# Value products of an attention kernel: parts of values side by side, parts of probabilities in one stream, row sums on VectorE

## The reference

```
lat = layer_norm(latents, ln_lat_g, ln_lat_b)
ctx = layer_norm(context, ln_ctx_g, ln_ctx_b)
q = (lat @ Wq).reshape(b, n, HEADS, DHEAD).transpose(0, 2, 1, 3)
kv = ctx @ Wkv
k, v = jnp.split(kv, 2, axis=-1)
...
k = apply_rope(k, cos[None, None], sin[None, None])
attn = jnp.einsum('bhnd,bhsd->bhns', q, k) * scale
attn = jnp.clip(attn, -11.0, 11.0)
attn = jax.nn.softmax(attn, axis=-1)
out = jnp.einsum('bhns,bhsd->bhnd', attn, v)
```

## Time and profile before

| | before |
|---|---|
| median of 3 runs | 1448.81 us (1445.45 to 1450.21) |
| profiled execution, its own time | 1454.4 us |
| its span in the profile | 1452.7 us |
| TensorE busy | 1394.5 us (96%) |
| VectorE busy | 850.0 us (59%) |
| ScalarE busy | 797.3 us (55%) |
| GpSimd busy | 833.6 us (57%) |
| TensorE's granted clock over the run | 0.98 |

### The profile page before, as it was taken

One profiled execution on the slowest core, in us unless ns is written; L12 is line 12 of the kernel. 1 busy time (PEld: TensorE's weight loads), 2 busy tenths in 40 slices (PEclk: granted clock), 3 DMA queues, 4 the chain that ended last, 5 costly groups with the idle time before them and its releaser, 6 DMA issues. The chain is left out here.

```text
span 1452.7 us, 25242 instructions
## 1 busy us (share of the span) xinstructions
PE 1394.5 (96%) x8758; PEld 1139.3 (78%) x8758; DVE 850.0 (59%) x1420; ACT 797.3 (55%) x1237; POOL 833.6 (57%) x723
## 2 busy tenths in 40 slices
PE   5899999999999999999999999999998889999998
PEld 3578888888788888878888888888887566766664
DVE  6456565666466566655565666656554356657564
ACT  3356566665566665656666656656555312346652
POOL 3267677776667776766777777777765324110002
PEclk9999999999999999999999999999999989899999
DMA  7567766766666676656677666776767380369994
GB/s 241 178 118 130 123 118 110 132 116 135 114 120 123 111 130 110 139 100 129 113 131 122 123 130 118 130 123 107 138 107 163 116 326 0 131 219 365 357 370 150
DMA packets 115219, 218.44 MB, mean 150 GB/s; under 512 B 13312, under 2 KB 49152, under 8 KB 108928
## 3 DMA queue, kind: packets, MB, share of 16 engines
q1 hardware_dynamic: 111920, 209.00, 63.8%
q0 software_dynamic: 1280, 4.20, 0.9%
q10 hardware_dynamic: 1872, 3.41, 0.6%
HBM read 132.67 MB, written 16.78 MB: 103 GB/s over the span
## 5 line engine op out<-in xcount | busy, mean ns | idle before, releaser
L605 POOL TENSOR_TENSOR p_parts<-probs,p_parts 128x512 fp32r<-128x512 f32 x256 | 340.3, 1349 | 252.2 <-ACT p_parts L660 252.2
L660 ACT ACTIVATE p_parts<-probs 128x512 fp32r<-128x512 f32 x256 | 147.7, 625 | 245.5 <-PE banks L914 237.9
L768 DVE TENSOR_TENSOR probs<-banks,probs 128x1024 f32<-128x1024 f32 x128 | 156.7, 1224 | 164.1 <-ACT probs L668 164.1
L709 ACT ACTIVATE probs<-probs 128x1024 f32<-128x1024 f32 x128 | 135.9, 1062 | 142.6 <-POOL probs L612 142.5
L866 PE MATMUL banks<-wv_hi,x_hi 128*128 128x512 f32 x512 | 208.5, 407 | 4.9 <-PEq L170 4.9
L867 PE MATMUL banks<-wv_lo,x_hi 128*128 128x512 f32 x512 | 202.8, 396 | 0.0
L881 PE MATMUL banks<-x_hi,wk_hi 128*128 128x512 f32 x512 | 201.8, 394 | 0.0
L868 PE MATMUL banks<-wv_hi,x_lo 128*128 128x512 f32 x512 | 201.8, 394 | 0.0
L883 PE MATMUL banks<-x_hi,wk_lo 128*128 128x512 f32 x512 | 199.6, 390 | 0.0
L882 PE MATMUL banks<-x_lo,wk_hi 128*128 128x512 f32 x512 | 199.3, 389 | 0.0
L910 PE MATMUL banks<-p_parts,v_hi 128*65 128x128 f32 x1024 | 192.0, 224 | 0.6 <-POOL p_parts L605 0.6
(11 more groups left out here) (291 smaller groups left out, 2694.5 us busy)
## 6 DMA issues: line engine op xcount, KB each, us to landing
queries<-q_scratch SPq DMA_DIRECT2D x256, 128.0 KB, 6.0
keys<-wo_room SPq DMA_DIRECT2D x128, 256.0 KB, 5.6
keys<-turned_odd SPq DMA_DIRECT2D x128, 256.0 KB, 5.6
row_room<-in_ctx SPq DMA_DIRECT2D x64, 256.0 KB, 6.2
wo_room<-in_down SPq DMA_DIRECT2D x10, 1024.0 KB, 7.1
wo<-in_gate SPq DMA_DIRECT2D x8, 1024.0 KB, 8.2
gate_raw<-in_up SPq DMA_DIRECT2D x8, 1024.0 KB, 10.2
up_raw<-in_gate SPq DMA_DIRECT2D x7, 1024.0 KB, 8.2
```

Of the source, the lines that this page charges most:

```text
L605: nc.gpsimd.tensor_tensor(p_parts[:, 1, j, :], probs[:, pair % 2, j, :], p_parts[:, 0, j, :].bitcast(F32), ALU.subtract).then_inc(p_lo_rea ...
L768: nc.vector.tensor_tensor(mine, ps_s[:, :, :, 0, :].rearrange("p j i n -> p (j i) n"), mine, ALU.add).then_inc(s_taken, 1)
```

## The change

- `weigh`: the high and low parts of a head's values stand side by side in `v_parts` (128 weight columns), and the high and low parts of the probabilities of one row tile stand side by side in `p_parts` (256 moving columns). One product gives all four combinations; `sums` now fills the whole bank: rows 0 to 63 come from high values, rows 64 to 127 from low ones, columns of `w` 0 from high probabilities and of `w` 1 from low ones. 24 products of 128 columns become 8 of 256. The column of ones is gone.
- `add_values` is two instructions: all 128 rows of the high probabilities' columns, then, behind the first one's semaphore, the upper 64 rows of the low ones' columns. Low x low is left out as before.
- `add_totals`, new on VectorE: `tensor_reduce` over the four row tiles of `probs` (1024 values in, 256 out, read in steps of 128 values), ahead of `take_scores`; behind `take_scores`, except in a batch's first chunk, an addition of 256 columns into `totals`.
- `turn_sums`: four transposes of 128x128 (totals and sums of two heads) for two of 65x65. `finish`: two reductions of 256 values each, then the reciprocal and the two scalings; they wait for each other.
- ScalarE's copy of the scores (L668) also waits for the totals of the pair two before, whose `probs` it overwrites.
- SyncE: 2 query slots for 4; each step loads the queries of one pair, behind the scores of step t - 4; the early loads of the last batch stand behind the query load and wait for one more semaphore. One constant and one copy of the setup are gone; `attn_third` lies in room of `x_hi`.

The second addition and the reduction stand ahead of the taking of the scores, the addition of the totals behind it. The diff, cut to its core:

```
@@ attend, buffers
-        v_lo = sb("v_lo", [P, ROW_TILES, HEADS, DHEAD], F32R)
-        p_parts = sb("p_parts", [P, 2, 2, CHUNK], F32R)
-        acc = sb("acc", [DHEAD + 1, HEADS, QUERIES])
+        p_parts = sb("p_parts", [P, 2, ROW_TILES, 2, QUERIES], F32R)
+        acc = sb("acc", [2 * DHEAD, HEADS, QUERIES])
+        totals = sb("totals", [P, HEADS, QUERIES])
+        fresh = sb("fresh", [P, 2, QUERIES])
-        sums = ps_o[0:DHEAD + 1, 0:2 * QUERIES].rearrange("p (j n) -> p j n", n=QUERIES)
+        sums = ps_o.rearrange("p (j w n) -> p j w n", j=2, n=QUERIES)
-        turned_sums = ps_s[:, 0, 0:2, 0, 0:DHEAD + 1]
+        turned_sums, turned_totals = ps_s[:, 0, 0:2, 0, :], ps_s[:, 0, 0:2, 1, :]
@@ sync, step
+                if exists(b, t - 2):
+                    if exists(b, t - SCORE_LAG):
+                        wait_alone(sp, s_ready, b * BSTEPS + (t - SCORE_LAG + 1))
+                    load_queries(b, t - 2)
...
-                    for pair in (t - 3, t - 2):
-                        if exists(b, pair) and exists(b, t - 2):
-                            load_queries(b, pair)
@@ scalar, step
                     wait(act, p_lo_ready, b * (2 * BSTEPS) + (2 * pair - 2))
+                    wait(act, totals_ready, b * BSTEPS + (pair - 1))
@@ vector, add_values
-                        nc.vector.tensor_tensor(mine, sums, mine, ALU.add).then_inc(o_added, 1)
+                        nc.vector.tensor_tensor(mine, sums[:, :, 0, :], mine, ALU.add).then_inc(o_added, 1)
+                    wait(dve, o_added, 2 * n + 1)
+                    nc.vector.tensor_tensor(below, sums[0:DHEAD, :, 1, :], below, ALU.add).then_inc(o_added, 1)
+            def add_totals(b, pair, part):
+                if exists(b, pair):
+                    n = b * BSTEPS + pair
+                    m = pair % STEPS
+                    mine = totals[:, 2 * m:2 * m + 2, :]
+                    first = pair // STEPS % CHUNKS == 0
+                    if part == 0:
+                        wait(dve, probs_ready, n + 1)
+                        out = nc.vector.tensor_reduce(mine if first else fresh[:], probs[:, pair % 2].rearrange("p j (i n) -> p j n i", n=P),
+                                                      AX_X, ALU.add)
+                        out.then_inc(totals_ready if first else fresh_ready, 1)
+                    elif not first:
+                        wait(dve, fresh_ready, fresh_until(b, pair) + 1)
+                        nc.vector.tensor_tensor(mine, mine, fresh[:], ALU.add).then_inc(totals_ready, 1)
@@ vector, finish
-                    nc.vector.reciprocal(recip[:], turned_sums[:, :, DHEAD]).then_inc(recip_ready, 1)
+                    nc.vector.tensor_reduce(total[:], turned_totals, AX_X, ALU.add)
+                    nc.vector.tensor_reduce(there, turned_sums.rearrange("p j (w e) -> p j e w", w=2), AX_X, ALU.add).then_inc(whole_ready, 1)
+                    wait(dve, whole_ready, done + 1)
+                    nc.vector.reciprocal(recip[:], total[:]).then_inc(recip_ready, 1)
@@ vector, step
+                add_totals(b, t - VALUE_LAG, 0)
                 take_scores(b, t - SCORE_LAG)
+                add_totals(b, t - VALUE_LAG, 1)
@@ tensor, turn_sums
+                    wait(pe, totals_ready, b * BSTEPS + (pair + 1))
                     for j in range(2):
-                        tr = nc.tensor.transpose(turned_sums[:, j, :], acc[:, 2 * (pair % STEPS) + j, :],
-                                                 keep["ident"][0:DHEAD + 1, 0:DHEAD + 1])
+                        nc.tensor.transpose(turned_totals[:, j, :], totals[:, 2 * (pair % STEPS) + j, :], keep["ident"][:])
+                    for j in range(2):
+                        tr = nc.tensor.transpose(turned_sums[:, j, :], acc[:, 2 * (pair % STEPS) + j, :], keep["ident"][:])
@@ tensor, weigh
-                            nc.tensor.matmul(sums[:, j, :], v_hi[:, i, 2 * m + j, :], p_parts[:, 0, j, cols],
-                                             start=(i == 0), stop=False)
-                            nc.tensor.matmul(sums[0:DHEAD, j, :], v_lo[:, i, 2 * m + j, :], p_parts[:, 0, j, cols],
-                                             start=False, stop=False)
-                            mm = nc.tensor.matmul(sums[:, j, :], v_hi[:, i, 2 * m + j, :], p_parts[:, 1, j, cols],
-                                                  start=False, stop=(i == ROW_TILES - 1))
+                            mm = nc.tensor.matmul(sums[:, j], v_parts[:, i, 2 * m + j], p_parts[:, j, i],
+                                                  start=(i == 0), stop=(i == ROW_TILES - 1))
```

## The result

The changed kernel takes **1580.26 us** (median of 4 runs, 1574.44 to 1583.87), the kernel before 1449.51 in the same comparison: a ratio of 1.0898 with an interval of 1.0845 to 1.095. The forecast was 1421, the range ended at 1482. The change is slower, by more than rivals 1 and 2 allowed for.

What follows compares the result with a forecast made beforehand. TensorE's order was taken as the bound, busy 96% of the span. Terms -57.6 (products), +7 (transposes), +13 (scores), +10 (wait for the normalised tile) gave -28 us: 1421 for the median, range 1400 to 1482.

Steps and rivals of the forecast that it cites:

- rivals 1 and 2: Strided reduction slower than 1.22 us: 1467 us at 1.8 (chance 0.32), or 1512 to 1544 at double, 2.36 (chance 0.12).
- The value products: TensorE's `weigh`: eight wider products take 1.00 us for 1.45, 0.45 less a pair over 128 pairs, -57.6 us.
- The transposes: TensorE's `turn_sums`: four transposes of 128x128 for two of 65x65, with the product behind them, 32 times, +7 us.
- VectorE's additions, the reduction's price: VectorE, each step: second addition, reduction and totals added; the reduction taken at 1.22 us, between 1.22 and 2.36.
- The ring to L134: Clip, exponential, tile power, normalising, TensorE's tile transposes: margin 1.15 shrinks to 0.04, wait 0.2 in 48 double steps, +10 us.
- When the scores are taken: VectorE takes scores 0.21 us later, TensorE reaches `turn_sums` 0.45 earlier: wait of 0.5 us, 32 times, +13 us.
- no bound by its sum: VectorE's total work fits: 13.6 us in a double step of 15.4, 16.3 in one of 17.3 that turns sums.
- Rival 1: Strided reduction takes e us over 1.22, so -28 + 80e and the change is slower; 1467 us, chance 0.32.
- Rival 3: Keys' last DMA lands late, its margin of 2.6 us shrinking to 0.8: 1430 to 1442 us; chance 0.08.
- At no cost: `finish`, ScalarE's wait for totals, the high and low parts' new places, query loads and the shorter setup add nothing.

Runs made afterwards that it cites:

- adjacent: The changed kernel with its reduction reading four neighbouring values instead of steps of 128, so the row sums are of other elements; 1474.28 us.
- no_totals: The changed kernel without row sums (no reduction, no addition of totals), all else kept; 1455.38 us.
- nt_power: The changed kernel without row sums, with GpSimd's power of a context tile moved to the head of its even step; 1421.38 us.
- nt_early: The changed kernel without row sums, GpSimd's tile power at the head of its even step, VectorE's normalising at the end of its even step; 1418.39 us.
- early: The whole changed kernel, GpSimd's tile power at the head of its even step, VectorE's normalising at the end of its even step; 1496.25 us.
- before_adjacent: The kernel before plus a reduction of 1024 adjacent values into an unread spare tile, ahead of the taking of scores; 1445.45 us.
- late: The changed kernel with the reduction and the addition of totals both moved behind `finish`; 1574.81 us.

## Why the forecast was wrong, point by point

- **The value products**: right in kind, 0.51 us a pair instead of 0.45, so -65 for -57.6. The eight products take 0.94 and the forecast had 1.00.
- **The transposes**: +8 for +7.
- **VectorE's additions, the reduction's price**: mis-sized, and the first step that failed. 1.22 us by the only row of this operation, measured 2.00 (1.95 ns a value against 1.18 for adjacent ones). `adjacent` changes nothing but the distance of the reads, and that decided. The stride alone is 106 us here, 38 in the kernel before. The Trainium skill's figure for two-source programs that hop ("Vector Engine (DVE) Microarchitecture Reference", section 5.2), which makes an estimate of 1.8 us, was nearer than the row and still 0.2 low.
- **The ring to L134**: the step that failed most. The forecast had a wait of 0.2 us in each double step, "between 0 and 16", and 0.25 for a longer clip; measured were some 2 us in each of 48. 0.2 are the forecast's, 0.8 are the reduction and 0.9 is L126 itself, priced at its old 0.55. The forecast had seen that the clip loses time to VectorE's instruction with two inputs, and looked at this place only from one side: who is slowed besides GpSimd, and who starts first behind L120, was not asked. The trace of before had the rows for it: L605 waiting 0.33 for its high parts while L126 starts 0.29 ahead of it. no_totals shows the ring without the reduction (48 us of waits at L134), nt_power takes these away with one instruction moved.
- **When the scores are taken**: the wait at the turned sums came, +44 for +13. Here the sentence "no bound by its sum" is what failed. The forecast gave VectorE 16.3 us in a double step that turns sums; it works in 19.7 of 20.0. Twice 0.8 are the reductions, and the rest is L756, L758 and the scalings at 1.35, 1.52 and 0.99 us beside GpSimd.
- **Rival 1** was the right mechanism (a slow strided read) at the wrong size: with the measured e of 0.78 its formula gives -28 + 62 = +34, so 1483. The change is another 97 slower. Its 80 us for each us of delay leave out that a delay costs the port, and then the clock: `adjacent` gives 106 us for 0.79, 134 for each us.
- **The clock** had no term. 23 stretches of some 1.6 us are 38, less the 5 of before: +33.
- **Rival 3**, the keys: it came as 15 us in nt_early and 41 in `early`, where other waits no longer cover it; in the change itself 6.8.
- **At no cost** were said to be `finish`, the waits of ScalarE and the query loads. For the loads no wait of TensorE shows up; `finish` is not free, since it belongs to the 19.7.
- One reading would have changed the forecast: VectorE's idle time ahead of the scores is 164.1 us in the kernel before. I counted the copy as no longer last after the change, but not what that idle time was for the old kernel, a cover of 1.28 us a step, which before_adjacent shows to be whole. The change spends it three times: ScalarE's copy comes earlier, the second addition takes 0.34, the reduction 2.0.

## What to carry to other kernels

Where two engines exclude each other at a port, the one that starts first goes at full rate, so look at every instruction that is released by the other engine: if the releaser's next instruction is ready too, the released one runs behind it (0.56 us became 1.27 to 1.5). Put such a releaser early in its queue, well ahead of the need; here one 0.55 us instruction moved gave 34 us without and 59 us with the row sums. And price a strided read by a run of its own size and stride before building on it: an idle gap covers 1.2 us for nothing, while 2.0 us through the same gap cost 38.

## What the runs showed of the hardware

- A reduction of 1024 float32 to 256 takes 1.205 us with adjacent reads and 1.99 to 2.05 in the mean with a step of 512 bytes. GpSimd's work beside it changes this by at most some 0.1 us.
- A scaling of 512 columns (L126) takes 0.55 us alone and 1.2 to 1.5 when a GpSimd instruction of 1.3 us has begun 0.05 to 0.4 us earlier. The later it comes, the shorter it is: 1.48 at 0.07, 1.28 at 0.30, 1.17 at 0.42, 0.69 at 0.88, so it ends some 1.55 to 1.6 us after that instruction's start each time, as if it had to wait for its end. Additions of 512 columns with both inputs in SBUF take 0.68 and up to 1.5, of 256 columns 0.42 and up to 1.55 (`late`). Those with one input in PSUM stay the same (L794 1.21, L803 0.68).
- Products of 256 columns with weights of 128 start 0.118 us apart, of 130 columns 0.15, of 66 columns 0.08, of 128 columns with weights of 64 or 65 0.06.
- After waits of 2 to 3 us in otherwise unbroken work TensorE was granted 1.2 GHz for some 3.4 us in 23 steps of the changed kernel, and not in others with the same wait (2.90 both ways in the windows above).
